# Causal attention and a squared-ReLU layer on one core: score units of equal width, 18 steps per batch, value products between the scores

## The chip, the core and the metric

The kernel runs on one core of a Trainium2 chip. The core has a matrix engine (TensorE, PE in the profile; its weight loads are PEld), a vector engine (VectorE, DVE), a scalar engine (ScalarE, ACT), a general engine (GpSimd, POOL), and a queue that issues the transfers (SyncE, SP). Each runs its own list of instructions in order and waits on semaphores for the others. The metric is device time in microseconds, median of three runs: 2451.49 us before (2451.22 to 2463.14).

## The reference

Sixteen batches of 1024 tokens with 256 channels. The output is the input, plus attention, plus a spiking feed-forward part, both of the normalised input:

```python
def _L0_attn_ref(x, ...):                 # x: (16, 1024, 256), 16 heads of 16
    Q = x @ Wq.T + bq                     # K and V alike
    Q = _rope(Q, pos)                     # K too: even and odd channels rotated
    scores = einsum('bhqd,bhkd->bhqk', Q, K) * scale
    scores = where(causal, scores, NEG_INF)
    attn = einsum('bhqk,bhkd->bhqd', softmax(scores), V)
    return concat @ Wo.T + bo

def _L0_ffn_ref(x, W_fc, W_proj):
    h = square(relu(einsum('bsd,fd->bsf', x, W_fc)))      # 1024 hidden channels
    y = einsum('bsf,df->bsd', h, W_proj)
    # five steps of a leaky neuron with reset: the number of spikes / 5
    ...

xn = _layernorm(x)
x = x + attention(xn) + feed_forward(xn)
```

## The kernel before

**Numbers.** Products that need full precision are split: a float32 operand is a "hi" part (fp32r) and a "lo" part, the rest, and three fp32r products (hi·hi, lo·hi, hi·lo) are summed in PSUM (`split_product`, L960 to L965). The products of exponentials and values, and the output product, are plain float32.

**Tiles.** For a batch the attention goes through four "quads" of four heads. In a quad, a unit `(kt, g)` is 128 keys (`kt`, 0 to 7) against up to 512 queries (half `g`, 0 or 1), from the diagonal on. Causality leaves twelve units: six 512 queries wide, and two each of 384, 256 and 128, together nine times 512. For each unit TensorE makes the scores of two head pairs in two PSUM pairs (`scores`, L1132; slots `pair0`, `pair1`), ACT takes the exponential of each pair into an SBUF buffer `probs` (`weigh` of ACT, L603, two instructions), POOL masks the triangle on diagonal units (`mask`, L525), and TensorE multiplies with the values, which carry a column of ones for the denominator (`weigh` of TensorE, L1148). The sums of a half of a quad stand in one PSUM bank, `pv_bank`, and DVE copies them out (`take_numer`, L848) before the next half may start in it.

**Order.** Each engine has a function `interval` that runs over the same steps `n`. An interval does the attention of batch `b` and, in the same steps, the projections, rotations and feed-forward of batch `b+1`, and the output product of batch `b-1`. There are 17 intervals: one without attention ahead (the prologue), 15 with both, a last one with attention only. Twelve of them are a hardware loop. What stands in which step is written by hand in the tables from L63 on. Before, there are 25 steps per interval; in step `n` TensorE makes the scores of unit 2n, then other work of the step, then the scores of unit 2n+1, then the value products of units 2n-2 and 2n-1.

**Other work.** `T_AT`: transposes; `QK_AT`: query and key projections (`query_key`), rotated by DVE (`rotate`), summed by POOL (`sum_qk`, L504), split by ACT and DVE (`high_qk`, `low_qk`) and stored to DRAM by SP (`store_planes`, L292), from where `ring` (L302) loads them in head order, 13 transfers for a quad; `V_AT`: value projections; `O_AT`: the output product of the batch before, to which DVE adds the rest (`finish`); `EXPAND_AT` and `CONTRACT_AT`: the sixteen hidden blocks. A hidden block goes through TensorE `expand` (L1088), ACT `rectify`, DVE `activate_h` (square and round), POOL `h_low`, TensorE `contract` (L1104).

**Buffers.** Four `probs` buffers taken in turn, three hidden-block buffers `h_hi` and `h_lo`, two `h_sq`. `bank_a`, `bank_b`, `bank_c` of PSUM serve all other work in turn.

## Time and profile before

| | us |
|---|---|
| median of three runs | 2451.49 |
| the profiled execution's own time | 2449.72 |
| its span, first to last instruction | 2447.9 |
| TensorE busy | 2274.3 (93%) |
| ScalarE busy | 1471.0 (60%) |
| VectorE busy | 1454.9 (59%) |
| GpSimd busy | 1072.5 (44%) |
| TensorE's share of the chain that ended last | 75% |

Busy time of TensorE counts from an instruction's start to its modelled end, and instructions overlap; what a block of matmuls costs is read from the start of its first to the start of the next block's first. A row of the timeline can merge several instructions of one form (x4, x16); a float32 matmul shows as two records.

### The profile page before, as it was taken

What the parts mean: (1) busy time and instruction counts of PE and PEld (TensorE: products, weight loads), DVE (VectorE), ACT (ScalarE), POOL (GpSimd) and SP (SyncE); (2) the same over time, 40 slices, a digit from 0 to 9 for tenths busy, and PEclk for the clock granted to TensorE, in tenths of its full rate; (3) what the DMA queues carried; (4) which work ended last, traced back from release to release, by engine and by line L of the source; (5) the groups of instructions that cost most, each with busy time, mean ns of one, the idle gap of its engine ahead of it and who ended that gap; (6) DMA issues with size and microseconds to landing.
All of it is one profiled execution on the core that took longest, in us unless ns stands there. A gap on an engine that the chain in (4) does not pass through costs nothing.

```text
span 2447.9 us, 50277 instructions
## 1 busy us (share of the span) xinstructions
PE 2274.3 (93%) x16260; PEld 1402.7 (57%) x16260; DVE 1454.9 (59%) x2108; ACT 1471.0 (60%) x2053; POOL 1072.5 (44%) x1065
## 2 busy tenths in 40 slices
PE   3799999999999999999999999999999999999975
PEld 2656656556656556656556655656555555665522
DVE  6667565665646567465665656567475666755421
ACT  2176666656666666665656666566665656566662
POOL 3455353444535445353444535455353444534320
PEclk9999999999999999999999999999999999999987
DMA  4333443535445263443535444263444536344432
GB/s 142 109 123 97 112 147 88 164 90 156 119 112 157 64 192 93 119 140 88 166 90 158 116 129 141 63 192 93 133 126 105 158 90 170 106 118 132 105 97 56
DMA packets 167717, 297.28 MB, mean 121 GB/s; under 512 B 25008, under 2 KB 112816, under 8 KB 155056
## 3 DMA queue, kind: packets, MB, share of 16 engines
q1 hardware_dynamic: 167472, 294.01, 42.1%
q8 instruction: 155, 2.54, 0.4%
q14 instruction: 90, 0.74, 0.1%
HBM read 173.32 MB, written 102.76 MB: 113 GB/s over the span
## 4 chain that ended last, share of the span: by engine, by line
PE 75%; ACT 8%; DMA 5%; DVE 5%; issue 5%; POOL 1%; ACTq 0%; SPq 0%; DVEq 0%; POOLq 0%
PE pair L964 26%; PE pair L1159 18%; PE pair L1125 16%; PE pair L1142 14%; ACT probs L610 6%; DMA recip_rows<-recip_dram 4%; DMA recip_dram<-denom 1%; ACT planes L585 1%; DVE h_sq L810 1%; DVE attn L755 1%; ACT h_sq L601 1%; DVE shift L782 0%; PE pair L977 0%; DVE bound_max L768 0%; DVE denom L750 0%
## 5 line engine op out<-in xcount | busy, mean ns | idle before, releaser
L610 ACT ACTIVATE probs<-pair 128x1024 f32<-128x1024 f32 (+3 forms) x1536 | 1155.9, 814 | 397.6 <-PE pair L1142 394.9
L529 POOL TENSOR_SCALAR_AFFINE_SELECT probs<-probs 128x512 f32<-128x512 f32 x512 | 376.3, 739 | 851.7 <-ACT probs L610 851.0
L1142 PE MATMUL pair<-q_ring,k_ring 64*128 64x512 f32 (+3 forms) x3072 | 528.9, 406 | 77.8 <-ACT probs L610 53.2
L1159 PE MATMUL pair<-probs,v_sb 128*17 128x512 f32 (+3 forms) x6144 | 578.2, 494 | 20.9 <-DVE numer L857 20.9
L1142 PEld LDWEIGHTS pair<-q_ring,k_ring 64*128 64x128 f32 x3072 | 246.6, 185 | 468.0 <-ACT probs L610 240.9
L523 POOL TENSOR_TENSOR h_lo<-h_sq,h_hi 128x512 fp32r<-128x512 f32 x256 | 365.6, 1428 | 271.0 <-DVE h_hi L820 271.0
L601 ACT ACTIVATE h_sq<-pair 128x512 f32<-128x512 f32 x256 | 153.4, 599 | 463.9 <-PE pair L964 463.9
L810 DVE TENSOR_TENSOR h_sq<-h_sq 128x512 f32<-128x512 f32 x256 | 185.0, 723 | 308.4 <-ACT h_sq L601 308.3
L1125 PE MATMUL pair<-wproj_hi,h_hi 128*128 128x256 f32 x1024 | 313.8, 306 | 12.3 <-POOL h_lo L523 10.3
L1159 PEld LDWEIGHTS pair<-probs,v_sb 128*17 128x17 f32 x6144 | 142.1, 97 | 297.6 <-issue 223.3
L834 DVE SCALAR_TENSOR_TENSOR count<-y_sb,count 128x512 bf16<-128x512 f32 x256 | 294.7, 1151 | 6.6
L1125 PE MATMUL pair<-wproj_hi,h_lo 128*128 128x256 f32 x1024 | 289.8, 283 | 0.0
L1125 PE MATMUL pair<-wproj_lo,h_hi 128*128 128x256 f32 x1024 | 289.4, 283 | 0.0
L507 POOL TENSOR_TENSOR rot<-rot,rot_b 128x1024 f32<-128x1024 f32 x64 | 167.5, 2617 | 191.3 <-DVE rot_b L739 191.3
L1125 PEld LDWEIGHTS pair<-wproj_hi,h_hi 128*128 128x128 f32 x1024 | 194.6, 190 | 79.2 <-issue 54.4
L964 PE MATMUL pair<-xT_hi,wfc_hi 128*128 128x512 f32 x512 | 209.4, 409 | 11.1 <-DVE rot_b L739 11.1
L964 PE MATMUL pair<-xT_hi,wfc_lo 128*128 128x512 f32 x512 | 202.8, 396 | 0.0
L964 PE MATMUL pair<-xT_lo,wfc_hi 128*128 128x512 f32 x512 | 199.8, 390 | 0.0
L1125 PEld LDWEIGHTS pair<-wproj_lo,h_hi 128*128 128x128 f32 x1024 | 195.3, 191 | 0.1
L1125 PEld LDWEIGHTS pair<-wproj_hi,h_lo 128*128 128x128 f32 x1024 | 195.0, 190 | 0.0
L715 DVE TENSOR_TENSOR xT_lo<-pair,xT_hi 128x512 fp32r<-128x512 f32 x64 | 41.4, 687 | 201.4 <-ACT xT_hi L575 201.4
L820 DVE CAST h_hi<-h_sq 128x512 fp32r<-128x512 f32 x256 | 145.0, 566 | 25.7
(87 smaller groups left out, 2690.3 us busy)
## 6 DMA issues: line engine op xcount, KB each, us to landing
qk_dram<-planes SPq DMA_DIRECT2D x128, 512.0 KB, 3.8
q_ring<-qk_dram SPq DMA_DIRECT2D x384, 128.0 KB
k_ring<-qk_dram SPq DMA_DIRECT2D x384, 128.0 KB
xn<-in_x SPq DMA_DIRECT2D x16, 1024.0 KB, 7.3
rs<-in_x SPq DMA_DIRECT2D x64, 256.0 KB, 2.8
acc_dram<-rs SPq DMA_DIRECT2D x64, 256.0 KB, 2.3
attn<-numer SPq DMA_DIRECT2D x256, 64.0 KB, 2.3
recip_rows<-recip_dram SPq DMA_DIRECT2D x32, 512.0 KB
```

Of the source, the lines that this page charges most:

```text
L507: pool.tensor_tensor(rot[u % 2][:, :, :], rot[u % 2][:, :, :], rot_b[u % 2][:, :, :], ALU.add).then_inc(rot_sum, 1)
L523: pool.tensor_tensor(h_lo[i % HB][:, :], h_sq[i % 2][:, :], h_hi[i % HB][:, :].bitcast(F32), ALU.subtract).then_inc(h_lo_done, 1)
L529: pool.affine_select(view, view, [[0, 4], [1, P]], ALU.is_ge, 0.0, base=0, channel_multiplier=-1).then_inc(mask_done, 1)
L601: act.activation(h_sq[i % 2][:, :], fc_bank[i], ACT.Relu).then_inc(relu_done, 1)
L610: act.activation(probs[n % NPB][:, 2 * pr:2 * pr + 2, 0:w], pair[m % NSLOT][:, :, 0:w], ACT.Exp, scale=SCALE).then_inc(exp_done, 1)
L810: dve.tensor_tensor(h_sq[i % 2][:, :], h_sq[i % 2][:, :], h_sq[i % 2][:, :], ALU.mult).then_inc(sq_h, 1)
L820: dve.tensor_copy(h_hi[i % HB][:, :], h_sq[i % 2][:, :]).then_inc(h_hi_done, 1)
L834: dve.scalar_tensor_tensor(count[:, :], y, edges[s], count[:, :], ALU.is_gt, ALU.add).then_inc(spike_step, 1)
L964: ins = pe.matmul(bank, lhsT, rhs, start=n == 0, stop=n == len(parts) - 1)
L1125: ins = pe.matmul(proj_bank[half][:, a * D:(a + 1) * D], h[i % HB][:, cols], w[:, f, :], start=f == 0 and n == 0 and a == 0, stop=f == NFT ...
L1142: ins = pe.matmul(pair[m % NSLOT][:, half, 0:width(n)], k_ring[rows, slot, pr, kt * P:(kt + 1) * P], q_ring[rows, slot, pr, q0:(g + 1) * G ...
L1159: ins = pe.matmul(pv_bank[32 * i:32 * i + VW, q0 - g * G:G], v_sb[:, kt, 4 * quad + i, :], probs[n % NPB][:, i, 0:width(n)], start=first, ...
```

## The change

Units become rows of segments that fill 512 columns: (1,0) with (3,0), (2,0) with (6,1), (5,1) with (7,1). A quad has nine units, each takes two full-width exponentials, and an interval has 18 steps. The value products no longer follow both scores of a step but stand as "runs" (`RUNS`) between the scores of unit 2n and those of unit 2n+1, in 16 of the 18 steps; the last run of a batch stands in step 0 of the next interval. There are five `probs` buffers, taken by a table `BUFFER`, and four sets of hidden-block buffers, in which `h_lo` overwrites `h_sq`. To make room, the low part of the rotated planes overwrites `rot` instead of a second half of `planes`; so `rotate` of u = 2, 3 now waits until the stores of u = 0, 1 have landed (`planes_out`). Hidden blocks, projections and output products stand in other steps, and the last batch's output product uses four banks. In the prologue the splitting of the later weights (`low_weight`) stands in step 4, behind the rotation of u = 2 and ahead of `low_qk` 1, where it stood in step 5.

The diff, cut to its core:

```diff
-UNITS = [(0, 0), (3, 0), (2, 0), (1, 0), (0, 1), (7, 1), (6, 1), (5, 1), (4, 1), (1, 1), (2, 1), (3, 1)]
+UNITS = [((0, 0),), ((1, 0), (3, 0)), ((2, 0), (6, 1)), ((0, 1),), ((4, 1),), ((5, 1), (7, 1)), ((1, 1),), ((2, 1),),
+         ((3, 1),)]
-NPB = 4
-NPAIR = NUNIT // 2
-NSTEP = NPAIR + 1
-HB = 3
+NSTEP = NUNIT // 2
+HB = 4
+RUNS = {2: ((0, 0), (1, 0), (1, 1), (2, 0)), 3: ((3, 0), (4, 0)), 4: ((5, 0), (5, 1), (6, 0)), 5: ((7, 0), (8, 0), (2, 1)),
+        6: ((9, 0), (10, 0), (10, 1), (11, 0)), 7: ((12, 0), (13, 0)), 8: ((14, 0), (14, 1), (15, 0)),
+        9: ((16, 0), (17, 0), (11, 1))}
+RUN_AT = {n + h * NSTEP // 2: [(u + 2 * NU * h, seg) for u, seg in run] for h in range(2) for n, run in RUNS.items()}
+LAST_RUN = RUN_AT.pop(NSTEP)
...
-INVERT_LAST, DIVIDE_LAST, INVERT_AT, DIVIDE_AT = 1, 3, 14, 17
-STATS_AT = {12 + n: (2 * n, 2 * n + 1) for n in range(NT // 2)}
-VAR_AT, ROOT_AT = 16, 17
+DIVIDE_LAST, INVERT_LAST, INVERT_AT, DIVIDE_AT = 3, 1, 11, 14
+BIAS_HERE_AT, BIAS_NEXT_AT = 7, 14
+STATS_AT = {10: range(0, 4), 11: range(4, 8)}
+VAR_AT, ROOT_AT = 11, 12
...
             def store_planes(nb, d, u):
-                for lo in range(2):
-                    sp.dma_start(qk_dram[d, is_k, lo, :, :, g * G:(g + 1) * G].rearrange("e p s -> p e s"),
-                                 planes[u % 2][:, lo, :, :].bitcast(F32)).then_inc(planes_out[u % 2], 16)
+                for lo, src in enumerate((planes[u % 2][:, :, :].bitcast(F32), rot[u % 2][:, :, :])):
+                    sp.dma_start(qk_dram[d, is_k, lo, :, :, g * G:(g + 1) * G].rearrange("e p s -> p e s"), src
+                                 ).then_inc(planes_out[u % 2], 16)
...
             def rotate(nb, u, eo, att):
                     if u >= 2:
-                        dve.wait_ge(rot_sum, nb * 4 + u - 1)
-                        dve.wait_ge(sq_done, nb * 4 + u - 1)
-                        dve.wait_ge(plane_lo, nb * 4 + u - 1)
+                        dve.wait_ge(planes_out[u % 2], (nb * 2 + 1) * 2 * 16)
...
             def scores(b, n, last):
-                    for half in range(2):
-                        ins = pe.matmul(pair[m % NSLOT][:, half, 0:width(n)],
+                    for seg, (kt, g) in enumerate(UNITS[n % NU]):
+                        to, q0 = column(n, seg), first_query(kt, g)
+                        for half in range(2):
+                            ins = pe.matmul(pair[m % NSLOT][:, half, to:to + width(kt, g)],
...
             def interval(b, att, last, more, norm, first=False):
                 for n in range(NSTEP):
-                    if att and n < NPAIR:
+                    if att:
                         scores(b, 2 * n, last)
-                    for i in CONTRACT_AT.get(n, ()) if more else ():
-                        contract(b, nb, i, last)
+                    if last and n == 0:
+                        run(b - 1, LAST_RUN, last)
+                    if att and n in RUN_AT:
+                        run(b, RUN_AT[n], last)
+                    for m in V_EARLY.get(n, ()) if att else ():
+                        values(b, m)
+                    if att:
+                        scores(b, 2 * n + 1, last)
...
+                    if more and n in EXPAND_AT:
+                        expand(b, nb, EXPAND_AT[n], last)
+                    for i in CONTRACT_AT.get(n, ()) if more else ():
+                        contract(b, nb, i, last)
+                    if more and n in EXPAND_LATE:
+                        expand(b, nb, EXPAND_LATE[n], last)
-                    if att and n < NPAIR:
-                        scores(b, 2 * n + 1, last)
-                    for m in (2 * n - 2, 2 * n - 1) if att and n else ():
-                        weigh(b, m, last)
...
+            def last_output(b):
+                run(b, LAST_RUN, True)
+                pe.wait_ge(attn_done, (b + 1) * KD)
+                for n in range(4):
+                    multiply_out(end_bank[n], b, n)
```

**TensorE, in the first interval with attention, from the norms on.** Before (`pair<-q_ring,k_ring` are scores, `pair<-probs,v_sb` value products, `wfc` expansions, `squares,sel` the norms):

```order
L1056 MATMUL pair<-squares,sel 32x512 x8
L1142 MATMUL pair<-q_ring,k_ring 128x128 x4
L1159 MATMUL pair<-probs,v_sb 17x256 x4
L1159 MATMUL pair<-probs,v_sb 17x384 x4
L1142 MATMUL pair<-q_ring,k_ring 128x256 x4
...
L1142 MATMUL pair<-q_ring,k_ring 128x384 x4
L1159 MATMUL pair<-probs,v_sb 17x512 x4
L1159 MATMUL pair<-probs,v_sb 17x128 x4
L1142 MATMUL pair<-q_ring,k_ring 128x512 x4
```

Now, in the same place:

```order
L1171 MATMUL pair<-probs,v_sb 17x512 x8
L1154 MATMUL pair<-q_ring,k_ring 128x512 x4
L1068 MATMUL pair<-squares,sel 32x512 x8
...
L1154 MATMUL pair<-q_ring,k_ring 128x512 x4
L1171 MATMUL pair<-probs,v_sb 17x384 x4
L1171 MATMUL pair<-probs,v_sb 17x128 x4
L1171 MATMUL pair<-probs,v_sb 17x512 x4
L1154 MATMUL pair<-q_ring,k_ring 128x512 x4
```

In both, score blocks and product blocks alternate with the other work; the blocks are now wider and fewer, and a product block carries 1024 columns here where it carried 640.

**GpSimd, same interval, from the sum of u = 3 on.** Before (`probs<-probs` are masks, `rs<-rs,bo_sb` the bias, `h_lo` the low part of a hidden block):

```order
L507 TENSOR_TENSOR rot<-rot,rot_b 128x1024
L529 AFFINE_SELECT probs<-probs 128x4x128 x3
L523 TENSOR_TENSOR h_lo_49<-h_sq_55,h_hi_52 128x512
L529 AFFINE_SELECT probs<-probs 128x4x128
L523 TENSOR_TENSOR h_lo_50<-h_sq_56,h_hi_53 128x512
L502 TENSOR_TENSOR rs<-rs,bo_sb 128x256 x4
L529 AFFINE_SELECT probs<-probs 128x4x128 x2
```

Now:

```order
L535 TENSOR_TENSOR rot<-rot,rot_b 128x1024
L553 AFFINE_SELECT probs<-probs 128x4x128
L545 TENSOR_TENSOR h_lo_57<-h_sq_49,h_hi_53 128x512
L530 TENSOR_TENSOR rs<-rs,bo_sb 128x256 x4
L553 AFFINE_SELECT probs<-probs 128x4x128 x2
L545 TENSOR_TENSOR h_lo_58<-h_sq_50,h_hi_54 128x512
```

Between the sum of u = 3 and the two masks behind the bias stood two hidden blocks and four masks; now one of each.

**VectorE, same interval, around the variance of the next input.** Before (`numer<-pair` is the copy that frees the bank of the value products):

```order
L846 COPY y_sb<-pair 128x512 x2
L810 TENSOR_TENSOR h_sq_56<-h_sq_56 128x512
L820 CAST h_hi_52<-h_sq_56 128x512
L695 TENSOR_TENSOR mean_gap<-stats 128x8
...
L703 SCALAR_TENSOR_TENSOR var<-mean_gap,var 128x8
L810 TENSOR_TENSOR h_sq_55<-h_sq_55 128x512
L820 CAST h_hi_53<-h_sq_55 128x512
```

Now:

```order
L780 RECIPROCAL denom<-denom 64x128
L857 SCALAR_TENSOR_TENSOR count<-y_sb,count 128x512 x2
L862 SCALAR_TENSOR_TENSOR rs<-count,rs 128x512
L722 BN_STATS stats<-xn 128x6 x4
L728 TENSOR_TENSOR mean_gap<-stats 128x8
...
L736 SCALAR_TENSOR_TENSOR var<-mean_gap,var 128x8
L880 COPY numer<-pair 128x512
```

The copy of `numer` now stands in one step behind the reciprocal, half of a spike count, four statistics and the whole variance; before, the variance stood between two hidden blocks.

## Rows read from the trace of the kernel before

**Rows 1.** Windows: length; busy PE, PEld, DVE, ACT, POOL (instructions); clock, DMA share, GB/s.
```profile
119.01:2301.32 2182.31, 2103.72 (x15209) 1298.97 (x15208) 1346.36 (x1937) 1370.90 (x1920) 996.15 (x984) 1.00 0.43 123
2301.32:2447.90 146.58, 101.39 (x692) 47.17 (x688) 28.08 (x36) 73.85 (x100) 27.07 (x37) 0.86 0.35 91
```

**Rows 2.** Timeline of TensorE during batch 7: start, length, instructions merged.
```profile
1241.00 0.73 PE L1142 MATMUL pair<-q_ring,k_ring 64*128 64x512 f32 x4
1241.66 1.91 PE L1159 MATMUL pair<-probs,v_sb 128*17 128x512 f32 x16
...
1244.17 0.39 PE L1125 MATMUL pair<-wproj_hi,h_hi 128*128 128x256 f32 x1
1244.39 0.28 PE L1125 MATMUL pair<-wproj_lo,h_hi 128*128 128x256 f32 x1
1244.51 0.27 PE L1125 MATMUL pair<-wproj_hi,h_lo 128*128 128x256 f32 x1
...
1247.17 0.44 PE L1142 MATMUL pair<-q_ring,k_ring 64*128 64x128 f32 x4
1247.54 1.91 PE L1159 MATMUL pair<-probs,v_sb 128*17 128x512 f32 x16
1249.38 0.50 PE L1142 MATMUL pair<-q_ring,k_ring 64*128 64x256 f32 x4
```

**Rows 3.** Waits of TensorE in the fifteen full intervals: total us, times, longest.
```profile
PE pair L1142 <- ACT probs L610: 29.1, 91, 1.1
PE pair L1142 <- issue: 24.0, 12, 2.3
PE pair L1159 <- DVE numer L857: 20.9, 15, 1.5
```

**Rows 4.** Timeline of the last interval and the start of the tail, TensorE.
```profile
2352.15 1.27 PE L1159 MATMUL pair<-probs,v_sb 128*17 128x256 f32 x16
2353.35 0.74 PE L1142 MATMUL pair<-q_ring,k_ring 64*128 64x512 f32 x4
...
2356.38 1.91 PE L1159 MATMUL pair<-probs,v_sb 128*17 128x512 f32 x16
...
2411.97 5.32 PE L1159 MATMUL pair<-probs,v_sb 128*17 128x512 f32 x32
```

**Rows 5.** Timeline of the same stretch, ScalarE: four exponentials in a row.
```profile
2353.95 3.77 ACT L610 ACTIVATE probs<-pair 128x1024 f32<-128x1024 f32 x4 [0.45 <-PE pair L1142]
```

**Rows 6.** Timeline of GpSimd during batch 8: the bias.
```profile
1339.71 3.67 POOL L502 TENSOR_TENSOR rs<-rs,bo_sb 128x256 f32<-128x256 f32 x4
```

**Rows 7.** Window over one variance of VectorE: length, its busy time, clock, DMA.
```profile
1384.05:1386.95 2.90, 2.83 (x8) 1.00 0.30 85
```

**Rows 8.** The page's groups: total us, mean ns | idle before, and what ended it.
```profile
L523 POOL TENSOR_TENSOR h_lo<-h_sq,h_hi 128x512 fp32r<-128x512 f32 x256 | 365.6, 1428 | 271.0 <-DVE h_hi L820 271.0
L601 ACT ACTIVATE h_sq<-pair 128x512 f32<-128x512 f32 x256 | 153.4, 599 | 463.9 <-PE pair L964 463.9
L810 DVE TENSOR_TENSOR h_sq<-h_sq 128x512 f32<-128x512 f32 x256 | 185.0, 723 | 308.4 <-ACT h_sq L601 308.3
...
L834 DVE SCALAR_TENSOR_TENSOR count<-y_sb,count 128x512 bf16<-128x512 f32 x256 | 294.7, 1151 | 6.6
...
L820 DVE CAST h_hi<-h_sq 128x512 fp32r<-128x512 f32 x256 | 145.0, 566 | 25.7
```

**Rows 9.** A group of VectorE by form, read alike.
```profile
L689 DVE BATCH_NORM_STATS2 stats<-xn 128x6 f32<-128x256 f32 x128 | 46.5, 406 | 6.5 <-DMA xn<-in_x 6.5
```

**Rows 10.** Window behind a loop end, columns as in rows 1.
```profile
1282.50:1285.90 3.40, 3.40 (x17) 3.31 (x16) 0.00 (x0) 2.23 (x3) 0.64 (x1) 0.50 0.48 79
```

**Rows 11.** The 128 stores of rotated planes (L299), all of SP.
```profile
DMA to landing us min/median/max: 2.8/3.8/5.5
```

**Rows 12.** Timeline of the prologue, VectorE.
```profile
43.29 2.83 DVE L667 TENSOR_TENSOR wv_lo<-wv_in,wv_hi 128x512 fp32r<-128x512 f32 x1
...
50.84 0.74 DVE L735 SCALAR_TENSOR_TENSOR rot<-pair,bqk_sb,table 128x512 f32<-128x512 f32 x1
```

470 lines of the change are left out of this document (234 added, 236 removed).

## The prediction

> **What bounds the kernel now.** I read the table of engines first, then windows that cut the run where the attention of a batch begins, then TensorE's timeline inside one interval, and last its waits. The windows show that 2182.3 of the 2447.9 us are the fifteen full intervals, 145.5 us each, with TensorE busy 2103.7 of them at clock 1.00, ScalarE 1370.9, VectorE 1346.4 and GpSimd 996.2 [rows 1]. So an interval is TensorE's list, read start to start, and a gain has to shorten this list or take a wait out of it. The last interval and the tail (146.6 us) are another regime: TensorE is busy 101.4 us at clock 0.86, and the exponentials set the pace [rows 1, 4, 5].
>
> TensorE's timeline shows that blocks have a fixed cost beside their columns. A score block 512 wide takes 0.66 us to the next block, one 128 wide 0.37 [rows 2]; four times the columns for 1.8 times the price. Interpolated, 256 costs 0.47 and 384 costs 0.56. A product block of 1024 columns takes 1.84 (1247.54 to 1249.38), one of 640 takes 1.20 (2352.15 to 2353.35), so a column costs 1.667 ns and a block 0.13 us beside [rows 2, 4]. And the first contraction matmul behind scores takes 0.22 to the next, the second 0.12 [rows 2]: coming back to ordinary products costs 0.1; leaving them I price the same.
>
> **Part 1, fewer and wider blocks (interval).** No matmul is dropped and no column either: twelve units and nine rows of segments are both nine times 512 per quad.
> Score blocks before, per quad: 6 x 0.66 + 2 x 0.56 + 2 x 0.47 + 2 x 0.37 = 6.76, per interval 27.0. Now 24 plain blocks are 15.84. The 12 mixed ones (384 with 128, 256 with 256) are not in the trace. From below they cost a plain block, 0.66; from above two separate blocks, 0.93 or 0.94. I take 0.68, since the block's fixed part is paid once: 24.0. Gain 3.0, with the ends 3.2 and 0.
> Product blocks: 24 become 16, 8 x 0.13 = 1.1, neither end off by more than 0.2, as the price is measured.
> Stretches of other work between attention blocks: 25 become 20 (18 steps, and the value products or a hidden block that stand early in steps 1 and 10). 5 x 0.2 = 1.0.
> Together 5.1 us, from 1.9 to 5.5.
>
> **Part 2, waits that go.** In the fifteen intervals TensorE sits idle 29.1 us in 91 waits for exponentials and 20.9 us in 15 waits for the copy of `numer` [rows 3], 3.3 us per interval. The first kind appears where a product block of 1.20 us is shorter than the two exponentials behind it (four take 3.77 [rows 5], 0.94 each); every run is now at least 1.84 and mostly starts behind a 0.66 block. The second goes because groups now end where a run ends, and the copy has until the next step. Each wait also costs a drained pipeline (the 0.1 above, on both sides). I count 4.0 as gone, between 2 and 4.6. The 2.0 us at the loop end (24.0 in 12 [rows 3]) stay.
>
> **Part 3, waits that come.** What is late next is on GpSimd and VectorE, at two places.
> (a) The masks of unit 14 (two segments, both diagonal), which the run in step 8 opens with. On GpSimd they stand behind `h_low` 0 and four bias adds. From the end of expansion 0 in step 6 TensorE needs, to reach that run, scores 0.68, run 1.84, scores 0.66, the norms (eight matmuls, 1.0 at 0.12 each), expansion 1.5 (a contraction and an expansion together take 3.00, 1244.17 to 1247.17 [rows 2]) and scores 0.66: 6.3 us. The other way: about 0.5 until ScalarE has done its share of u = 3, relu 0.6, square 0.7, round 0.6, low part 1.4 [rows 8], bias 3.67 [rows 6], two masks some 1.3 (estimated as the low part of a hidden block, the nearest row of GpSimd): 8.8. A wait of 2.5. It is 0 if TensorE reaches the run later than by my count, held up elsewhere, and 4 to 5 if the rotation chain below is late. Behind the waiting product stand all of TensorE's later blocks.
> (b) The copy of `numer` in step 11, which the run of step 12 waits for. From the end of expansion 6: scores 0.66, run 2.27 (1280 columns), scores 0.68, a hidden block in and two out (1.5 + 3.0), scores 0.66: 8.8 us. VectorE: relu 0.8 with its latency, square and round 1.3, then reciprocal (about 0.9), a half spike count 2 x 1.15 + 0.8 [rows 8], four statistics 1.6 [rows 9], the variance 2.9 [rows 7], the copy 0.7: 11.3. A wait of 2.5, from 1 to 4.
> (c) Step 2: scores of unit 5 behind transposed input on ScalarE, 0.5, from 0 to 1.
> (d) TensorE's clock. Behind a loop-end wait of some 2 us the granted clock was 0.50 in the stretch that followed [rows 10], that is 1.2 GHz instead of 2.4; TensorE was busy in all of its 3.4 us, so it cost half of that, some 1.6 us. The two waits of 2.5 are of this size: 3 us if both do it, 0 if neither; I take 0.8.
>
> **Part 4, the path through DRAM.** `rotate` of u = 2 and 3 now waits for the landing of the stores of u = 0 and 1, median 3.8 us, longest 5.5 [rows 11]. Queued behind it on VectorE are `finish`, `low_qk` and the copy of `numer`, for which TensorE waits. Laying steps 3 to 6 side by side, u = 2 rotates some 2 us before TensorE needs its bank, u = 3 about as late as the output product's bank comes free. I price it at 0, from 0 to 6.4 (the rival below).
>
> An interval: -5.1 - 4.0 + 2.5 + 2.5 + 0.5 + 0.8 = -2.8 us. Fifteen: -42. The first one also hands its last run (2.27) on: -2.
>
> **Part 5, last interval.** Before, from 2301.32 to the end of the last products at 2411.97 + 5.32 = 2417.29: 116 us. Two units 512 wide take 4.23 there (2352.15 to 2356.38), of which the four exponentials are 3.77 [rows 4, 5]. Now a run stands between the second exponential of one unit and the first of the next: run 1.84 or 2.27, scores 0.66, 0.6 until the exponential starts, and two exponentials of 0.94 with 0.1 on top: 4.8 or 5.2 for two units. Fifteen such steps 75, three steps with value products or no run 16, the last run behind the last exponential 2: 93. Gain 23, from 14 (if runs also wait for masks) to 30 (if exponentials hide the runs as before). The tail keeps its transfers: 0.
>
> **Part 6, prologue.** The splitting of the later weights takes from 43.29 to 50.84, 7.6 us [rows 12]. It now comes ahead of `low_qk` 1, whose store the rotation of u = 3 waits for, so that this rotation comes 9 to 11 us later. Four sets of hidden-block buffers for three then let the sixteen blocks run closer, by my count 9 us. +1, from -4 to +9.
>
> **The sum.** 1 - 42 - 2 - 23 = -66. The profiled execution took 2449.72, so 2383.7; the median of the runs shown is 1.8 above it: 2385 us.
>
> **Rivals.**
> Fewer new waits: GpSimd and VectorE run ahead of their places and (a), (b), (d) vanish. 15 x 5.8 = 87 less: about 2298. For it: both have 55 us free per interval or more [rows 1]. Against it: their lists are in order and what precedes is itself late.
> The clock falls behind every new wait: 15 x (3.0 - 0.8) = 33 more, 2418. For it, rows 10. Against it: most of TensorE's waits left the clock at 1.00 as the mean over the fifteen intervals shows [rows 1]. The Trainium skill, TensorE: Matmul & The Clock Gate, section HAM oscillation, says that gaps between bursts of matmuls send the array back to half clock and that a kernel can pay this in every round of its loop; by that rule the time would be this rival's.
> Half the wins fail (mixed blocks at two blocks' price, waits 1 us longer each): 15 x (3.0 + 1.1) = 62 more, 2447, no change.
> Slower: the DRAM path decides. If the two stores land in 5.5 instead of 3.8 (2 x 1.7), the transfers of `fin` ahead of them on SP cost another 1.5, and the clock falls behind the longer waits (1.5), an interval is 6.4 longer than forecast, 15 x 6.4 = 96: 2481. It turns into a loss from 4.4 us per interval on. For it: the two landings follow each other, and ring loads (13 transfers) use the same queue. Against it: TensorE reaches the two banks late enough by my count.
> That the change doesn't do what it says (units or runs elsewhere) the order excludes.
>
> **How the numbers follow.** Forecast 0.42 (its own range 2355 to 2410), fewer waits 0.22, clock 0.15, half the wins 0.08, DRAM path 0.13. The range is 2295 to 2445: it takes in the first four but for the lower tail of the second, and leaves most of the last. A measurement of this kernel tells 0.5%, 12 us, from no change: faster than 2439 has 0.79 of it (the first three), within 0.5% 0.08 with a little of the neighbours, slower 0.13.
>
> **What would show it.** Right: score blocks 512 wide still 0.66, mixed ones under 0.75; a last interval of about 93 us; TensorE waits of 2 to 3 us, once per interval for masks of POOL and once for `numer`; the prologue ends near 120. Wrong: mixed blocks near 0.93; a new wait for `rot` or `planes`; a clock of 0.50 in every interval; full intervals outside 139 to 146 us.

## The result, and the profile after

The changed kernel takes **2425.34 us** (median of four runs, 2423.38 to 2427.82) against 2452.51 us for the one before on the same chip: a ratio of 0.988, 95% interval 0.9851 to 0.991. So it is faster by 27 us (1.2%); 66 us were forecast. The sign was right and the time lies in the range, at two fifths of the size.

Its profiled execution, cut where the attention of batch 0 and that of the last batch begin (the answer to [rows 1], same columns):

```profile
127.72:2276.04 2148.32, 2035.83 (x15186) 1304.95 (x15186) 1318.46 (x1938) 1339.54 (x1560) 1031.65 (x984) 0.98 0.44 126
2276.04:2423.40 147.36, 104.40 (x713) 47.67 (x712) 27.41 (x38) 70.66 (x76) 24.61 (x37) 0.80 0.36 91
```

| us | before | after | difference | forecast |
|---|---|---|---|---|
| ahead of the first interval | 119.0 | 127.7 | +8.7 | +1 |
| fifteen full intervals | 2182.3 | 2148.3 | -34.0 | -44 |
| last interval and tail | 146.6 | 147.4 | +0.8 | -23 |
| span | 2447.9 | 2423.4 | -24.5 | -66 |

The two windows show how the 34 us come about. TensorE's busy time in the full intervals fell by 67.9 us, 4.5 each, although the clock fell from 1.00 to 0.98. Its idle time rose from 78.6 to 112.5 us. The waits of TensorE in that stretch (total, times, longest), the answer to [rows 3]:

```profile
PE pair L1171 <- DVE numer L880: 58.3, 28, 4.6
PE pair L1154 <- issue: 20.7, 12, 2.0
PE pair L1171 <- POOL probs L553: 10.7, 16, 1.2
PE pair L1154 <- ACT probs L640: 10.6, 25, 1.7
```

The exponentials cost 10.6 where they cost 29.1, as forecast. The copy of `numer` costs 58.3 where it cost 20.9. It is not the copy of step 11 that I had named: 14 of the 28 waits, 2.8 to 4.6 us each, stand at the run of step 7, in every full interval but the first. In one interval, on TensorE, SyncE and VectorE (start, length, instructions, idle before):

```profile
1322.50 1.99 PE L984 MATMUL pair<-wo_sb,attn 128*128 128x256 f32 x8
...
1326.00 0.80 PE L1154 MATMUL pair<-q_ring,k_ring 64*128 64x384 f32 x8
1331.21 3.61 PE L1171 MATMUL pair<-probs,v_sb 128*17 128x512 f32 x16 [4.41 <-DVE numer L880]
```
```profile
1317.35 0.37 SPq L334 DMA_DIRECT2D qk_dram<-rot  x1
1324.75 0.67 SPq L386 DMA_DIRECT2D denom<-numer  x1
1325.47 3.12 SPq L388 DMA_DIRECT2D attn<-numer  x4
1328.94 3.88 SPq L343 DMA_DIRECT2D q_ring<-qk_dram  x6
1333.00 3.81 SPq L343 DMA_DIRECT2D k_ring<-qk_dram  x6
...
1338.93 0.38 SPq L334 DMA_DIRECT2D qk_dram<-planes  x1
```
```profile
1330.46 0.69 DVE L880 COPY numer<-pair 128x512 f32<-128x512 f32 x1 [3.15 <-DMA attn<-numer]
```

Read them upward. The run of step 7 waits for the copy of quad 1's sums, since both use one bank. The copy waits until quad 0's sums have left `numer`. They are sent by `gather`, which for quad 0 first waits for all four output products of the batch before, so that SyncE stands from 1317.7 to 1324.75, until output product 3 is out of TensorE.

The held queue alone is not what the change brought. In the kernel before, the same gather stood in step 7 and waited for the same products, in the same batch from 1320.6 to 1329.37:

```profile
1325.39 3.72 PE L964 MATMUL pair<-wo_sb,attn 128*128 128x256 f32 x16
...
1341.77 1.27 PE L1159 MATMUL pair<-probs,v_sb 128*17 128x512 f32 x16 [1.37 <-DVE numer L857]
```

That is a hold of 8.8 us, longer than the 7.0 now, and the gather left 44.8 to 47.3 us behind the first value projection of its interval in all but the first, where it now leaves at 46.3 to 49.8. What moved is the reader: TensorE came to the run that needs quad 1's copy some 56 to 58 us into the interval and comes to it now some 48 to 52 us in (at 1326.8 in the rows above, 48.6 us behind 1278.16). From the issue of the gather to that run go 6.5 us (1324.75 to 1331.21); before there were 11 us for it, now there are 2.

Behind the wait, the run of 16 matmuls takes 3.61 us; the same shape takes 1.91 elsewhere [rows 2]. A window over it shows a granted clock near half, 1.2 GHz:

```profile
1330.00:1337.00 7.00, 5.79 (x27) 1.43 (x28) 3.45 (x5) 1.98 (x3) 4.11 (x4) 0.52 0.65 191
```

In the last interval (to be held against [rows 4, 5]) a run and the scores of two units take 6.54 us, 2354.24 to 2360.78, where 4.8 to 5.2 were forecast. ScalarE stands idle through most of each run, and the runs go at half clock:

```profile
2352.90 0.50 PE L1154 MATMUL pair<-q_ring,k_ring 64*128 64x512 f32 x2 [0.89 <-ACT probs L640]
2353.81 0.50 PE L1154 MATMUL pair<-q_ring,k_ring 64*128 64x512 f32 x2 [0.41 <-ACT probs L640]
2354.24 3.58 PE L1171 MATMUL pair<-probs,v_sb 128*17 128x512 f32 x16
...
2360.78 3.30 PE L1171 MATMUL pair<-probs,v_sb 128*17 128x384 f32 x24
```
```profile
2358.36 3.77 ACT L640 ACTIVATE probs<-pair 128x1024 f32<-128x1024 f32 x4 [2.77 <-PE pair L1154]
```

In the first preparation (to be held against [rows 12]) the rotation of u = 3 starts at 59.89, 9.05 us later. VectorE, with the low part of plane 1 (L775) behind the weights and each rotation behind a landing:

```profile
44.14 0.75 DVE L767 SCALAR_TENSOR_TENSOR rot<-pair,bqk_sb,table 128x512 f32<-128x512 f32 x1 [4.38 <-DMA qk_dram<-rot]
...
47.38 4.46 DVE L700 TENSOR_TENSOR wfc_lo<-wfc_in,wfc_hi 128x2048 fp32r<-128x2048 f32 x1
...
54.35 1.21 DVE L775 TENSOR_TENSOR rot<-rot,planes 128x1024 fp32r<-128x1024 f32 x1
59.89 0.75 DVE L767 SCALAR_TENSOR_TENSOR rot<-pair,bqk_sb,table 128x512 f32<-128x512 f32 x1 [4.33 <-DMA qk_dram<-rot]
```

### The profile page after: what moved, and what is told of

Same layout as the page of the kernel before. It is cut to its first block, busy times and chain, and to the rows that moved or that the text cites. A ratio compares the mean times of both kernels' runs of the same rounds, so it can differ in the third digit from the quotient of the medians.

```text
span 2423.4 us, 48395 instructions
## 1 busy us (share of the span) xinstructions
PE 2211.7 (91%) x16260; PEld 1410.4 (58%) x16260; DVE 1423.0 (59%) x2108; ACT 1436.5 (59%) x1669; POOL 1105.9 (46%) x1065
## 4 chain that ended last, share of the span: by engine, by line
PE 62%; DVE 10%; issue 8%; DMA 7%; SPq 6%; ACT 5%; POOL 2%; DVEq 0%; ACTq 0%; POOLq 0%
PE pair L984 23%; PE pair L1171 14%; PE pair L1135 13%; PE pair L1154 10%; DMA qk_dram<-rot 6%; ACT probs L640 3%; SPq L343 3%; DVE rot L775 3%; SPq L388 1%; DVE count L857 1%; SPq L334 1%; DVE stats L722 1%; DVE rot L768 1%; PE pair L996 1%; POOL probs L553 1%
## 5 line engine op out<-in xcount | busy, mean ns | idle before, releaser
L640 ACT ACTIVATE probs<-pair 128x1024 f32<-128x1024 f32 x1152 | 1115.3, 1026 | 588.1 <-PE pair L1154 587.8
L553 POOL TENSOR_SCALAR_AFFINE_SELECT probs<-probs 128x512 f32<-128x512 f32 x512 | 396.0, 793 | 527.6 <-ACT probs L640 527.6
L545 POOL TENSOR_TENSOR h_lo<-h_sq,h_hi 128x512 fp32r<-128x512 f32 x256 | 385.4, 1506 | 469.7 <-DVE h_hi L843 469.2
L1154 PE MATMUL pair<-q_ring,k_ring 64*128 64x512 f32 (+3 forms) x3072 | 450.6, 386 | 48.7 <-ACT probs L640 26.1
L1154 PEld LDWEIGHTS pair<-q_ring,k_ring 64*128 64x128 f32 x3072 | 229.6, 187 | 328.2 <-ACT probs L640 170.3
L1171 PEld LDWEIGHTS pair<-probs,v_sb 128*17 128x17 f32 x6144 | 155.0, 99 | 389.3 <-issue 282.6
L1135 PE MATMUL pair<-wproj_hi,h_hi 128*128 128x256 f32 x1024 | 293.3, 286 | 5.1 <-POOL h_lo L545 5.0
L984 PE MATMUL pair<-xT_hi,wfc_hi 128*128 128x512 f32 x512 | 222.4, 434 | 4.8 <-ACT h_sq L631 3.7
L1135 PEld LDWEIGHTS pair<-wproj_hi,h_hi 128*128 128x128 f32 x1024 | 195.9, 191 | 23.7 <-issue 10.9
L880 DVE COPY numer<-pair 128x512 f32<-128x512 f32 x128 | 87.9, 687 | 175.9 <-PE pair L1171 119.3
L775 DVE TENSOR_TENSOR rot<-rot,planes 128x1024 fp32r<-128x1024 f32 x64 | 148.8, 2325 | 1.9 <-ACT planes L615 1.9
```

The source lines that it names most:

```text
L545: pool.tensor_tensor(h_lo[i % HB][:, :], h_sq[i % HB][:, :], h_hi[i % HB][:, :].bitcast(F32), ALU.subtract).then_inc(h_lo_done, 1)
L553: ins = pool.affine_select(view, view, [[0, 4], [1, P]], ALU.is_ge, 0.0, base=0, channel_multiplier=-1)
L640: act.activation(probs[BUFFER[n]][:, 2 * pr:2 * pr + 2, :], pair[m % NSLOT][:, :, :], ACT.Exp, scale=SCALE).then_inc(exp_done, 1)
L775: dve.tensor_tensor(rot[u % 2][:, :, :].bitcast(F32R), rot[u % 2][:, :, :], planes[u % 2][:, :, :].bitcast(F32), ALU.subtract).then_inc(pl ...
L984: ins = pe.matmul(bank, lhsT, rhs, start=n == 0, stop=n == len(parts) - 1)
L1135: ins = pe.matmul(proj_bank[half][:, a * D:(a + 1) * D], h[:, cols], w[:, f, :], start=f == 0 and n == 0 and a == 0, stop=f == NFT - 1 and ...
```

## The experiments

All are edits of the changed kernel. "First" is the start of the first value projection of batch 0 in TensorE's timeline, "interval" the mean distance of the next fifteen, "rest" what follows the last of these starts to the end of the span. The ratio is to the kernel before, timed on the same chip, with its 95% interval; so ratios are compared across groups, not microseconds.

| kernel | median us | ratio | first | interval | rest |
|---|---|---|---|---|---|
| before | 2452.5 | 1 | 119.7 | 145.5 | 145.9 |
| changed | 2425.3 | 0.988 (0.985 to 0.991) | 130.8 | 143.3 | 143.7 |
| e_numer | 2418.1 | 0.984 (0.981 to 0.987) | 130.1 | 143.1 | 139.3 |
| e_fill_seven | 2439.0 | 0.992 (0.990 to 0.994) | 131.4 | 144.5 | 140.0 |
| e_fill_end | 2426.1 | 0.987 (0.985 to 0.990) | 131.4 | 143.2 | 142.2 |
| e_prologue | 2420.5 | 0.984 (0.982 to 0.986) | 126.0 | 143.5 | 142.8 |
| e_bias | 2419.8 | 0.986 (0.984 to 0.988) | 131.1 | 143.0 | 142.2 |
| e_numer_bias | 2423.1 | 0.987 (0.985 to 0.990) | 129.3 | 143.2 | 141.1 |
| e_fill_second | 2420.9 | 0.986 (0.984 to 0.988) | 129.3 | 143.2 | 140.8 |
| e_slots | 2409.5 | 0.982 (0.979 to 0.985) | 129.3 | 143.0 | 130.4 |
| e_order | 2428.3 | 0.988 (0.985 to 0.990) | 130.8 | 143.7 | 141.7 |
| e_hold | 2369.8 | 0.965 (0.963 to 0.967) | 131.1 | 140.0 | 135.2 |
| e_fill_first | 2414.0 | 0.983 (0.981 to 0.984) | 130.3 | 143.0 | 137.5 |
| e_best | 2408.7 | 0.981 (0.978 to 0.984) | 126.3 | 143.6 | 126.0 |
| e_hold_alone | 2385.2 | 0.970 (0.967 to 0.973) | 130.1 | 140.6 | 139.2 |
| e_banks | 2413.0 | 0.980 (0.977 to 0.984) | 125.7 | 142.9 | 142.9 |
| e_final | 2350.4 | 0.957 (0.954 to 0.959) | 124.2 | 139.9 | 122.9 |

The time and the last three columns are not from the same executions: first, interval and rest come from one profiled execution of each kernel. The interval is the number that no edit without the output products' move shortened by more than 0.4 us.

### Two buffers for the copy (e_numer)

```diff
-        numer = sb("numer", [P, S])
+        numer = sb("numer", [P, 2, S])          # by quad % 2, in the copy and in gather
-                if g == 0 and (last or quad):
+                if g == 0 and quad % 2 == 0 and (last or quad):
...
```

> Edit of the changed kernel: the copy of the value sums has two buffers, one for even quads and one for odd, so the copy of quad 1 no longer waits until quad 0's sums have been sent on to the attention buffer. Nothing else moves: SyncE is still held by the four output products before it sends quad 0's sums. Theory 1 (the wait of TensorE at the run of step 7, 63.5 us over the kernel, comes from this chain: output product 3 in step 6, SyncE held, the sending, the copy; the half clock behind it costs more): that wait falls from 4.4 us to under 1 in each interval, the stretch at half clock behind it goes, and the time falls by 4.4 + 1 to 1.5 us in 15 intervals and by 4 to 5 in the last one, 75 to 95 us, to 2330 to 2350. Rival (another wait stands right behind: the rotations or the sending of planes take its place): under 25 us, over 2400. Rival (the stretch at half clock is set off by something else): the wait goes but the half clock stays, about -65 us, 2360.

The wait at the run of step 7 fell from 4.4 to 1.17 us, and the interval stayed at 143.1. My theory was right on the wait and wrong on its worth. The time came up one step later:

```profile
1613.11 1.91 PE L1171 MATMUL pair<-probs,v_sb 128*17 128x512 f32 x16 [1.17 <-DVE numer L880]
...
1622.03 2.75 PE L1171 MATMUL pair<-probs,v_sb 128*17 128x384 f32 x24 [2.54 <-POOL probs L553]
```

The 2.54 us are the wait for the masks of unit 14 that the prediction had priced at 2.5. In 8 of the 14 intervals with this wait a half-clock stretch stands behind it (0.50 from 1623.0 to 1626.4 here), in the others none; so this edit saved part of the clock and gave the wait's length back. GpSimd shows what stands ahead of the two masks:

```profile
1617.31 2.81 POOL L530 TENSOR_TENSOR rs<-rs,bo_sb 128x256 f32<-128x256 f32 x4
1620.07 1.91 POOL L553 TENSOR_SCALAR_AFFINE_SELECT probs<-probs 128x512 f32<-128x512 f32 x2
```

### The wait filled with work (e_fill_seven)

```diff
+                    if last and more and n == 7:
+                        pe.wait_ge(rot_done, nb * 4 + 4)
+                        filler(16)              # 16 matmuls of 512 columns, result unused
                     if att and n in RUN_AT:
```

> Edit of the changed kernel: 16 matmuls of 512 columns with an unused result stand ahead of the run of value products in step 7 of the 14 full intervals from the second on, in the time in which TensorE waits there for the copy of the sums (4.4 us). The wait's end does not move. Theory (the wait itself is followed by 3.4 or 6.8 us at half clock, that is by a loss of 1.7 to 3.4 us of work): the half-clock stretch of each interval goes and the time falls by 14 x 1.5 to 3 us = 20 to 40 us. Rival (the clock there costs nothing, since the work behind it waits anyway, or the clock falls all the same): no change, within 8 us. If the 16 matmuls take longer than the wait, 14 times the excess is added, and the time rises.

The run behind the filling took 1.91 us in place of 3.61, so the half clock there follows the idle time and not the place. But the stretch did not go, and the kernel got slower, against my theory and the rival: in 13 of the 14 filled intervals a half-clock stretch stands some ten microseconds further on, behind a wait of 3.2 us at the run of step 8 for the masks of unit 14 (granted clock 0.58 from 1205 to 1209), and the interval grew by 1.2 us. That wait has three parts, seen in the interval of batch 7. The changed kernel waited 0.5 there already. TensorE came 1.45 us earlier, as its run went at full clock. And the masks ended 1.2 us later, because the bias took 3.25 us in place of 2.80 and the two masks 1.86 in place of 1.22:

```profile
1200.61 3.25 POOL L530 TENSOR_TENSOR rs<-rs,bo_sb 128x256 f32<-128x256 f32 x4
1203.83 1.86 POOL L553 TENSOR_SCALAR_AFFINE_SELECT probs<-probs 128x512 f32<-128x512 f32 x2
```

VectorE's work on the norms came 1.4 us earlier too and now stood beside them; that this is what stretched them is likely by the rows at the end of this document, but no run tests it.

### The bias moved, alone and with two buffers (e_bias, e_numer_bias)

```diff
-BIAS_HERE_AT, BIAS_NEXT_AT = 7, 14
+BIAS_HERE_AT, BIAS_NEXT_AT = 4, 14
```

> Edit of the changed kernel, a single number: GpSimd adds the bias to the residual of the second half in step 4 and not in step 7, where it stands ahead of the masks of unit 14. The copy of the sums keeps its one buffer, so the wait at the run of step 7 stays. Theory (two chains end within 4 us of each other in steps 7 and 8, and the one at the run of step 7 hides the masks almost wholly): the short wait at the run of step 8 goes, nothing else; the time falls by at most 15 x 0.5 = 8 us, to 2417 to 2427. Rival (the bias takes GpSimd from something that waits in the half-clock stretch): over 15 us less.

As expected, nothing that stands clear of the scatter: 64.2 us of waits for `numer` stayed.

> Edit of the changed kernel: two buffers for the copy of the sums, as in the run before, and the bias in step 4 and not in step 7. With two buffers alone the wait at the run of step 7 fell from 4.1 to 1.2 us, and 2.5 us of waiting for the masks of unit 14 came up one step later, the half clock with it: the interval stayed at 143.7 us. Theory (the masks are the next chain, by the 2.8 us of the bias ahead of them): with both edits the waits of steps 7 and 8 together are under 2 us and no stretch at half clock is left there, so each of 15 intervals loses 2.5 + 1 to 1.5 us, 50 to 60 us in all against two buffers alone, 2355 to 2370. Rival (a third chain, the exponentials of unit 14 behind the squares and planes of rotation 3 on ScalarE, or the low part of the hidden layer, ends at the same time): 2400 to 2415.

The rival's mechanism held, a third chain, though 2423 us lies above its 2400 to 2415. With waits of 1.17 and 0 at the two runs, a third one of 4.10 us came in step 9, and the interval stayed at 143.2:

```profile
PE pair L984 <- ACT h_sq L631: 56.1, 19, 4.1
```

Expansion 3 shares its bank with expansion 2, whose `rectify` writes over `rot[0]` and so waits until plane 2 has been stored. That store is issued behind the twelve ring loads (1328.94 to 1337 in the rows above), and these behind the held gather.

### The queue reordered (e_order)

The edits of `e_numer_bias` are in it too.

```diff
                     if att and n == 5:
                         gather(b, 0, last)
-                        load_ring(b, d, 2, b * 2 * NUNIT + 2 * NU)
...
                     if more and n in (6, 7):
                         store_planes(nb, nd, n - 4)
+                    if att and n == 7:
+                        load_ring(b, d, 2, b * 2 * NUNIT + 2 * NU)
```

> Edit of the changed kernel: two buffers for the copy of the sums and the bias in step 4, as in the run before, and in SyncE's order the storing of planes 2 and 3 ahead of the 12 loads of the third quad's ring, which are issued in 9 us. With the first two edits alone, 4.1 us of waiting stood in step 9: TensorE's third expansion for the rectifier, which waits for the landed store of plane 2, issued behind those loads and behind the output products that hold SyncE. Theory (three chains start at output product 3 and at rotation 3 and end within a microsecond of each other: copy of the sums, masks of unit 14, stored plane 2; taking away the last one shows the gain of all): no wait over 1.5 us is left in steps 7 to 9 and no half clock, and each of 15 intervals loses 4 + 1 to 1.5 us, 141 to 139 from 143.9: 60 to 85 us in all, 2340 to 2360. Rival (a fourth chain, the later ring or the stored plane 3): 2400 to 2415.

Again a fourth chain, as the rival has it: 143.7 us per interval, and with 2428 us the time lies above even the rival's range. The stores were early, and now the ring itself was late at the start of quad 2:

```profile
PE pair L1155 <- DMA q_ring<-shift_dram: 62.5, 15, 5.8
```

Four chains had now shown waits of some 4 us (the masks 2.5 to 3.2, the ring up to 5.8) within three steps of each other. Three of them (sums, stored plane, ring) run through SyncE behind the gather. To shuffle what stands behind a held queue only picks which of them is last.

### The output products earlier (e_hold, e_hold_alone)

```diff
-O_AT = {3: 0, 4: 1, 5: 2, 6: 3}
+O_EARLY, O_AT = {4: 1, 5: 3}, {3: 0, 4: 2}     # O_EARLY: ahead of the step's second scores
-        o_bank = (bank_a, bank_a, bank_a, bank_b)
+        o_bank = (bank_a,) * 4
```

`finish` of an early product stands ahead of the step's rotation, and expansion 0 waits for all four. In `e_hold` the bias is in step 4 too.

> Edit of the changed kernel with one buffer for the sums: output products 1 and 3 stand ahead of the second unit's scores of steps 4 and 5 and product 2 at the end of step 4, so that all four are done by about 38 us of the interval in place of 46, and SyncE is free that much earlier; the bias in step 4. Theory (the held queue is what the wait at the run of step 7 and the late store of plane 2 have in common): both waits go, without another buffer and without a new order of the queue; rotations 2 and 3 come 1.8 us later, and the interval loses 3 to 5 us, 2345 to 2375. Rival (the rotations, now later by 1.8 us, are what the masks and stores hang on): under 1.5 us per interval, 2395 to 2415.

The theory held: 140.0 us per interval, 2370 us. SyncE issues the gather as soon as plane 1 is stored and the sums are there, 6.7 us earlier in its interval than in the changed kernel (39.9 us behind the first value projection, there 46.6), and the wait for the copy is down to 3.2 us in the whole kernel:

```profile
1570.33 0.37 SPq L334 DMA_DIRECT2D qk_dram<-rot  x1
1571.04 0.67 SPq L386 DMA_DIRECT2D denom<-numer  x1
1571.77 2.97 SPq L388 DMA_DIRECT2D attn<-numer  x4
```

Not all is gone: the second scores of step 7 now wait up to 1.8 us for exponentials, and in 11 of the 15 intervals a half-clock stretch still stands 49 to 55 us in (granted clock 0.50 from 1443.5 to 1446.9).

> Edit of the changed kernel: the output products alone moved earlier (1 and 3 ahead of the second unit's scores in steps 4 and 5, 2 at the end of step 4); the bias stays in step 7, one buffer for the sums. With the bias in step 4 as well this gave 2370 us and intervals of 139.2 us. Theory (the held queue is the cause of the wait at the run of step 7 and of the late store of plane 2; the bias ahead of the masks of unit 14 is a chain of its own that ends 1.5 to 2.8 us later than the run wants it): this run stands between, some 1.5 to 3 us per interval above it, 2390 to 2415. Rival (the masks are no bound, since the run that wants them comes late anyway): 2366 to 2376, and then my forecast's price of 2.5 us for them was wrong in kind.

It came out at 2385, between the two ranges, so neither holds as stated. It does stand apart from `e_hold` (0.967 to 0.973 against 0.963 to 0.967, the two just touching; intervals 140.6 and 140.0), in the direction of the theory: the products' place is worth 2.6 us per interval, the bias 0.6, about the scatter of unedited intervals, with a wait that comes up here and is mostly gone in `e_hold` (2.2 us in all):

```profile
PE pair L1169 <- POOL probs L553: 15.2, 17, 2.6
```

### The last interval (e_fill_end, e_fill_second, e_fill_first, e_slots)

Three kernels put one matmul of 512 columns with an unused result ahead of score blocks where no later batch is prepared; they differ in where.

```diff
                     m = 2 * n + pr
+                    filler(fill)     # e_fill_end: all units from step 4; e_fill_second: each step's
                                       # second unit; e_fill_first: its first unit, from step 7
                     if m >= NSLOT or last:
```

> Edit of the changed kernel: in the last interval alone (no later batch to prepare), from step 4 on, one matmul of 512 columns with an unused result stands ahead of each of the four score blocks of a step, where TensorE waits for exponentials. It adds 56 matmuls of a fifth to two fifths of a microsecond, 12 to 24 us of TensorE's time, all of it in waits by the theory. Theory 1 (the last interval took 116 us and not the forecast 93 because TensorE's waits for exponentials set its clock to half, and a run of value products then takes 3.3 us in place of 1.84): the clock stays at 1.0 from step 4 to the end, a step takes 5.0 to 5.3 us in place of 6.4, and the time falls by 14 x 1.1 to 1.4 = 15 to 20 us. Rival (the pace is set by the exponentials and their buffers, and the clock is a consequence without a price): within 4 us. Rival (the added matmuls lie on the path): slower by 5 to 20 us.

> Edit of the changed kernel: in the last interval from step 4 on, one matmul of 512 columns with an unused result ahead of the two score blocks of each step's second unit alone, where TensorE waits 0.89 and 0.41 us for exponentials. With one ahead of all four blocks the clock stayed at 1.0 from 2340 us to the end and the runs took 1.84 to 2.28 us, but each added matmul took 0.43 us, so that two of the four in a step lay on the path, and the last interval fell by 1.5 us alone. Theory (the half clock that follows the waits costs 1.5 us in each run): now the clock is kept for nothing, a step takes 4.9 to 5.3 us in place of 6.5, and the last interval falls by 10 to 15 us. Rival (the clock is not kept with half the filling, or its price is not on the path): within 3 us.

> Edit of the changed kernel: in the last interval from step 7 on, one matmul of 512 columns with an unused result ahead of the two score blocks of each step's first unit, where TensorE waits 0.89 and 0.41 us. In the run with them ahead of the second unit they stood on the path (no wait there) and still the stretch from the run of step 7 to the last run fell from 64.1 to 58.3 us, at a clock of 1.0. Theory (half clock costs 1.5 us in each run of value products that follows a wait): the same stretch takes 53 to 56 us and the kernel is 8 to 11 us faster than the changed one. Rival (a wait for exponentials of the same length stands at the full clock): 62 to 65 us.

The first gained 1.5 us of the rest, the second 2.9, the third 6.2; `e_prologue` and `e_banks`, with no edit here, stand 0.9 below the changed kernel, so the first gain is hardly one. From the run of step 7 to the last whole run the changed kernel takes 64.1 us at clock 0.77, the second 58.4 at 0.97, the third 58.3 at 0.86, in this order:

```profile
2324.78:2388.86 64.08, 51.01 (x340) 17.04 (x340) 13.38 (x19) 37.93 (x41) 12.06 (x17) 0.77 0.29 80
```
```profile
2325.75:2384.10 58.35, 50.60 (x362) 19.23 (x362) 13.69 (x19) 38.27 (x41) 12.76 (x17) 0.97 0.32 88
```
```profile
2320.75:2379.05 58.30, 53.14 (x360) 19.57 (x361) 13.33 (x19) 38.19 (x41) 11.69 (x16) 0.86 0.33 88
```

So half clock does cost time here: the stretch is about 6 us shorter even with some twenty added matmuls in it. What the second kernel gains in the stretch it partly loses ahead of it, where its fillings of steps 4 to 6 stand: it comes to the run of step 7 3 us later. All three expectations for this interval (15 to 20, 10 to 15, and a stretch of 53 to 56) were too high. A filling matmul was not cheap: it takes 0.43 us beside scores, and makes the two score matmuls behind it take 0.43 too where they took 0.33.

> Edit of the changed kernel: in the last interval from unit 14 on the scores go through three pairs of banks in place of two (the third is free there, since the layer's other products are done), so that ScalarE has a block of scores in hand while TensorE multiplies values. Theory (my forecast of 93 us for that interval failed on two things: with two pairs ScalarE idles through each run of value products, and the waits that follow on TensorE bring half clock; both come from the number of pairs): a step takes 4.6 to 5.0 us in place of 6.3 to 6.5 in 10 steps, the clock stays at 1.0, ScalarE's idle time of 2.7 us a step falls under 1.3, and the time falls by 13 to 18 us, to 2407 to 2412. Rival (the runs wait for their own exponentials or for the copies of sums, whatever the scores' banks): under 4 us.

```diff
+THREE_FROM = 28
+def slot_of(m, ends):
+    return (0, 1, 3)[(m - THREE_FROM) % 3] if ends and m >= THREE_FROM else m % NSLOT
```

The theory held, at the low end, and this was the larger cause. The rest fell by 13.3 us to 130.4; two units and their run now take 3.95 (2345.44 to 2349.39), close to the four exponentials' 3.77, and the clock stays at 1.00 in this stretch:

```profile
2345.44 1.91 PE L1186 MATMUL pair<-probs,v_sb 128*17 128x512 f32 x16
2347.28 0.97 PE L1169 MATMUL pair<-q_ring,k_ring 64*128 64x512 f32 x6
...
2349.39 1.92 PE L1186 MATMUL pair<-probs,v_sb 128*17 128x384 f32 x24
```
```profile
2345.00:2355.00 10.00, 8.58 (x78) 3.19 (x82) 0.00 (x0) 9.63 (x11) 1.86 (x3) 1.00 0.48 136
```

ScalarE is busy 9.63 of 10 us. What the rest keeps is the 5.2 us wait at its step 7.

### The first preparation (e_prologue, e_banks)

```diff
-                    if first and n == 4:
+                    if first and n == 5:        # VectorE: low parts of the weights behind rotation 3
                         for w in range(1, 4):
```

> Edit of the changed kernel: in the first preparation alone, VectorE makes the low parts of the three other weights in step 5, behind the low part of plane 1 and the rotation of unit 3, and not in step 4, ahead of both. Theory (the start of the first interval came 9 to 10 us later than before because these three, 7.6 us of VectorE, now delay the low part of plane 1, its store and with that rotation 3, the norms and all behind them): rotation 3 comes 7 to 9 us earlier, TensorE's wait of 13.6 us for the squares shrinks to about 5, the first expansion waits some 3 to 5 us for the weights' low part instead, and the time falls by 5 to 9 us. Rival (the late start comes from the single bank for the expansions, where each waits some 0.75 us for the rectifier, and the planner's other moves): under 2 us of change.

First fell by 4.8 us, just below the theory's 5 to 9: rotation 3 came 7.9 us earlier, but the first expansion then waited for the weights' low part.

```profile
59.75 0.80 PE L984 MATMUL pair<-xT_hi,wfc_hi 128*128 128x512 f32 x1 [9.86 <-DVE wfc_lo L700]
```

> Edit of the changed kernel in the first preparation alone: the low parts of the weights behind rotation 3, and odd expansions go to a bank of the scores' first pair but one (free there), so that an expansion doesn't wait until the one before has been rectified. The weights alone brought the first values product of batch 0 from some 130.3 us (129.3 to 131.4 in seven runs) to 126.0. Theory (the rest of the 9 us is the single bank, 6 waits of 0.75 us): the first values product starts at 121 to 123 and the time falls by 8 us against the changed kernel. Rival (the hidden layer's pace there is set by GpSimd's low parts and VectorE, whose waits of 3.05 and 1.96 us at the end stay or grow): it starts at 125 to 127.

The rival held: 125.7 against 126.0, so the single bank is no cause. Its ratio of 0.980 is not explained by that; the intervals differ by 0.7 us from those of `e_prologue`, about what the mean interval scattered by where it was not edited (142.9 to 143.5 in seven kernels). What stays of the excess is in the rows above: rotation 2 waits 4.38 us for a landing at 44.14, where before it ran at 39.52 with no wait, as the low part then had a buffer of its own. No run takes this wait away, so that it is the rest of the excess is not shown.

### Together (e_best, e_final)

> All edits together: two buffers for the sums, bias in step 4, planes 2 and 3 stored ahead of the third ring, three pairs of banks for the scores from unit 14 of the last interval, the low parts of the weights behind rotation 3 in the first preparation. Theory (the gains lie in different stretches and add up): the time of the first run of this group less 13 us for the last interval and 5 for the preparation, 2320 to 2345 if the intervals lose 4 to 5.5 us. Rival (a fourth chain in the intervals): 2385 to 2400.

With `e_order`'s edits inside, the intervals stayed at 143.6 and only the two ends gained. That is the rival's mechanism; its 2385 to 2400 was still too low for the 2409 measured.

> The edits that each gained, together: output products earlier, bias in step 4, three pairs of banks for the scores from unit 14 of the last interval, the first preparation as in the run before. Theory (three different stretches, gains add): 2370 less 5 to 10 (first preparation) and less 8 to 13 (last interval, of which the output products have already given 3 to 4): 2347 to 2357, ratio to the kernel before of 0.956 to 0.960. Rival (the clock: less waiting in one place brings half clock in another): 2360 or over.

With `e_hold` in their place: **2350.4 us**, ratio 0.957 (0.954 to 0.959), the lower part of the range; the fastest of all, 4.3% under the kernel before. The gains add up: interval 139.9, rest 122.9. The largest wait of TensorE that remains:

```profile
PE pair L1167 <- ACT probs L653: 47.1, 52, 1.8
```

## Why the prediction was half right

**Part 1, blocks: right.** Mixed score blocks take 0.67 (256 with 256: 1677.56 to 1678.23) and 0.72 (384 with 128: 1674.57 to 1675.29), near the 0.68 taken and far from the two blocks' 0.93; a run of 1280 columns takes 2.27:

```profile
1674.57 0.79 PE L1154 MATMUL pair<-q_ring,k_ring 64*128 64x384 f32 x8
1675.29 2.34 PE L1171 MATMUL pair<-probs,v_sb 128*17 128x512 f32 x24
1677.56 0.74 PE L1154 MATMUL pair<-q_ring,k_ring 64*128 64x256 f32 x8
1678.23 0.50 PE L984 MATMUL pair<-xT_hi,wfc_hi 128*128 128x512 f32 x1
```

TensorE's busy time fell by 4.5 us per interval with the half-clock stretch included; 5.1 were forecast without it.

**Part 2, waits that go: right for the exponentials** (29.1 to 10.6 us), wrong for `numer`, which grew from 20.9 to 58.3. The sentence "The second goes because groups now end where a run ends, and the copy has until the next step" counted when the copy must be done and not when it may begin. It was right for the copies that wait for nothing else: the 14 waits away from step 7 came to 0.2 us each.

**Parts 3 and 4, waits that come: near in sum, wrong in place.** I forecast 4.0 us of waits gone and 5.5 new, a balance of 1.5; TensorE's idle time rose by 2.3 per interval. That these are near each other is luck: (b), the copy in step 11, and the rest came to little, and a wait that I did not have stood in their place. (a) was right to 0.1 us, but hidden behind that wait: only `e_numer` showed it. There is luck in it too. In `e_numer` both ways from the end of expansion 0 are 2.1 us longer than I counted, TensorE's 8.4 for 6.3 and the other 10.9 for 8.8 (the bias took 2.8 for 3.67, but ScalarE's share of u = 3 2.2 for 0.5, and the low part 2.2 for 1.4). The wait that counted, 4.4 us and a half-clock stretch at step 7, I did not have at all. The failed steps are the sentence on `numer` in part 2, quoted above, and the one in part 4 that priced the path through DRAM at 0 by "laying steps 3 to 6 side by side": I followed the stores and their landings, and not SyncE's own waits. The gather of quad 0 stands behind the last output product, leaves at the same time of the interval as before, and is now needed some 8 us earlier. The slower rival named this queue, with another mechanism. As a size the interval is near: -2.3 measured, -2.8 forecast.

**(d), the clock: right as a mechanism.** Each of the fifteen intervals has a half-clock stretch near step 7, some two or three. `e_fill_seven` showed that a run goes at full clock when TensorE has work in the wait ahead of it, and also that the stretch then comes up behind the next wait. The Trainium skill, TensorE: Matmul & The Clock Gate, section HAM oscillation, says that idle gaps between bursts of matmuls bring the array back to half clock; here the runs behind waits show it (3.61 us against 1.91).

**Part 5, the last interval: the largest miss, -23 forecast, +0.8 measured with the tail.** The failed step is the price of two units, 4.8 or 5.2 us, where 6.54 was measured; over fifteen steps of that length that is about the whole miss. Its terms, "run 1.84 or 2.27, scores 0.66, 0.6 until the exponential starts, and two exponentials of 0.94 with 0.1 on top", add up to 5.1 or 5.5, so some 4 us of the 23 were a wrong addition. The rest is in the terms: the step took the run at full clock, and it let ScalarE work beside the next scores. In the trace four exponentials (3.77) and a run (3.3 to 3.6 at half clock) hardly overlap, as ScalarE has no scores in hand during a run: it stood idle 2.77 us ahead of the four. `e_slots` gave 13.3 us of it back with a third pair of banks, the fillings some 6 with the clock; 5.2 are the wait at step 7, which `e_hold` removed from here as well.

**Part 6, the prologue: mis-sized, +1 forecast, +8.7 measured.** The delay of rotation 3 was forecast as 9 to 11 and was 9.05. The failed step is the return of 9 us through a fourth set of hidden buffers: it did not come. The prologue grew by nearly the whole delay. `e_prologue` took 7.9 us off the delay and returned 4.8; `e_banks` excludes the single bank as what eats the return. Why the fourth set brings nothing stays open.

## What to carry to other kernels

When a wait of some microseconds is removed and the time stays, look for the chains that end just behind it and ask what they share; here it was one semaphore wait in SyncE's in-order queue, and moving the four products that it waits for gave 44 us by the ratios (57 with the bias), where three repairs behind it (`e_numer`, `e_numer_bias`, `e_order`) gave 0 to 10. A wait that cost nothing before can cost after a change that leaves it alone: the queue was held as long in the old kernel, but its reader came 8 us later. So for each transfer behind a wait, write down when it leaves and when its result is first needed, before and after. Where an engine is paced by another, count the buffers between them before pricing an overlap.
